# When an edge sum's round reads its register values: needs behind the one-hot rows, places behind the node work

## The reference, cut to what matters

```
edge_index = stack([src, dst])              # 50000 edges, sorted by dst, dst = 50000 * u**2
x = ln(x + EdgeMLP(x))                      # segment_sum(mlp(x[src], x[dst]) * w, dst)          agg0
x = ln(x + Sage2(x))                        # segment_sum(h[src], dst) / deg, twice              agg1, agg2
x = ln(x + Gcn2(x))                         # segment_sum(h[src] * norm, dst), twice             agg3, agg4
x = ln(x + Attention(x))                    # segment_sum(v[src] * softmax_by_src, dest)         agg5
```

## Time and profile before

| | us |
|---|---|
| median of 3 runs | 7158.25 |
| profiled execution | 7164.57 |
| its span | 7162.9 |
| busy in the span: PE / DVE / ACT / POOL | 4883.4 / 4104.0 / 2723.8 / 4236.2 |
| first to last one-hot rows of agg0 | 1186 to 1600 |
| of agg1, agg2 | 1904 to 2426, 2439 to 2946 |
| of agg3, agg4 | 3293 to 3862, 3898 to 4413 |
| of agg5 | 6364 to 6902 |

### The profile page before, as it was taken

One profiled execution on the slowest core, in us unless ns is written; L12 is line 12 of the kernel. 1 busy time (PEld: TensorE's weight loads), 2 busy tenths in 40 slices (PEclk: granted clock), 3 DMA queues, 4 the chain that ended last, 5 costly groups with the idle time before them and its releaser, 6 DMA issues. The chain is left out here.

```text
span 7162.9 us, 132892 instructions
## 1 busy us (share of the span) xinstructions
PE 4883.4 (68%) x26557; PEld 3828.3 (53%) x26558; DVE 4104.0 (57%) x13488; ACT 2723.8 (38%) x6771; POOL 4236.2 (59%) x4642
## 2 busy tenths in 40 slices
PE   4666666779876666796787665766666767436667
PEld 2555554548654455685665554544444444325545
DVE  4555557887785432374454323866666666565448
ACT  1555555317642242495411422921111111113139
POOL 3777772004577777304766776467777777437740
PEclk7777778999997685798898866977777777667569
DMA  1222224649863233696775644932222222124358
GB/s 29 73 74 74 74 73 127 196 147 360 299 195 118 83 123 87 203 331 209 224 236 177 199 134 145 303 97 71 69 70 72 68 71 69 59 68 117 87 173 292
DMA packets 560382, 1016.38 MB, mean 142 GB/s; under 512 B 118514, under 2 KB 127120, under 8 KB 559888
## 3 DMA queue, kind: packets, MB, share of 16 engines
q1 hardware_dynamic: 243536, 444.87, 19.0%
q10 hardware_dynamic: 183456, 334.05, 13.5%
q0 software_dynamic: 133280, 236.29, 13.0%
HBM read 624.60 MB, written 390.17 MB: 142 GB/s over the span
## 5 line engine op out<-in xcount | busy, mean ns | idle before, releaser
L497 PE MATMUL agg_bank<-agg_msgs,agg_onehot 128*128 x7840 | 1404.1, 336 | 601.1 <-DVE agg_onehot L434 465.9
L497 PEld LDWEIGHTS agg_bank<-agg_msgs,agg_onehot 128*128 128x128 f32 x7840 | 1210.1, 236 | 852.9 <-issue 848.3
L434 DVE TENSOR_TENSOR agg_onehot<-iota,rel 128x512 f32<-128x512 f32 x1176 | 814.0, 692 | 1281.5 <-SPq L402 518.3
L356 POOL DMA_INDIRECT agg_msgs<-y,agg_rows x784 | 783.6, 999 | 294.1 <-issue 197.0
L534 ACT ACTIVATE agg_kept<-agg_bank,inv_root 128x128 f32<-128x128 f32 x784 | 223.4, 368 | 751.9 <-PE agg_bank L497 737.4
L534 ACT ACTIVATE agg_kept<-agg_bank,inv_deg 128x128 f32<-128x128 f32 x784 | 223.5, 368 | 693.0 <-PE agg_bank L497 666.4
L353 POOL DMA_INDIRECT agg_weight<-weights,agg_rows x392 | 406.8, 1038 | 127.0 <-issue 100.4
L497 PE MATMUL agg_bank<-agg_weighted,agg_onehot 128*128 x1568 | 338.1, 386 | 209.8 <-DVE agg_onehot L434 160.3
L1176 POOL DMA_INDIRECT mlp_xs<-in_x,mlp_rows x392 | 409.4, 1044 | 116.7 <-issue 115.8
L356 POOL DMA_INDIRECT agg_msgs<-near,agg_rows x392 | 395.1, 1008 | 122.3 <-issue 98.0
L1472 POOL DMA_INDIRECT by_source<-score_line,score_places x392 | 387.7, 989 | 127.3 <-issue 118.7
(11 more groups left out here) (334 smaller groups left out, 12457.6 us busy)
## 6 DMA issues: line engine op xcount, KB each, us to landing
sums<-agg_kept ACTq DMA_DIRECT2D x490, 256.0 KB, 2.1
agg_first<-y ACTq DMA_DIRECT2D x196, 256.0 KB
messages<-mlp_m SPq DMA_DIRECT2D x98, 256.0 KB, 2.1
agg_first<-in_x ACTq DMA_DIRECT2D x98, 256.0 KB
agg_msgs<-messages SPq DMA_DIRECT2D x98, 256.0 KB
l_z<-sums SPq DMA_DIRECT2D x98, 256.0 KB
x<-l_o POOLq DMA_DIRECT2D x98, 256.0 KB
near<-l_near_o SPq DMA_DIRECT2D x98, 256.0 KB
```

What stands on the lines that cost most here:

```text
L356: pool.indirect_dma_start(msgs[:, j, :], None, table[:, :], bass.IndirectOffsetOnAxis(ap=rows[:, third, j:j + 1], axis=0)).then_inc(sm[f"g ...
L434: nc.vector.tensor_tensor(onehot[:, j, :, :], k.iota[:, 0:P].unsqueeze(1).to_broadcast([P, Q, P]), k.rel[:, ds(i * (4 * Q) + j * Q, Q)].un ...
L497: t.matmul(bank[:, column[q], :], onehot[:, j, q, :], messages[:, slot[q], :], start=False, stop=True, skip_group_check=True)\
```

## The change

Two loads of registers stand at another place in the round.

- VectorE reads the needs of round n + 1 directly behind the one-hot rows of round n, in front of tally or node work, in all six edge sums. Round 0's are read ahead of the loop. So `needs` has one round more (16 bytes), is set to zero first, and everything allocated behind it starts 32 bytes later.
- PE, in agg3 alone, reads the places of round n + 1 behind the round's node step instead of ahead of it. In the other five sums it stays where it was.

```diff
+                c.link(v.memset(k.needs[0:1, :, :], 0))
...
-        def quads(eng, body, node_step, lag):
+        def quads(eng, body, node_step, lag, close=None):
...
                 for j in range(4):
                     body(i + FIRST_BESIDE, j)
                     node_step(i, j)
+                    if close is not None:
+                        close(i + FIRST_BESIDE, j)
...
-                def quad(i, j):
-                    dve.reg_load(words, k.needs[0:1, ds(i * 4 + j, 1), 0:len(words)])
+                def read_needs(at):
+                    dve.reg_load(words, k.needs[0:1, at, 0:len(words)])
                     for to, of in zip(least, words):
                         dve.reg_alu(to, of, 1, ALU.max)
+
+                read_needs(0)
+
+                def quad(i, j):
                     arrived = dve.snap(least[0], min_val=1, max_val=ET)
...
                         ALU.is_equal).then_inc(sm["onehot"], 1)
+                    read_needs(ds(i * 4 + (j + 1), 1))
...
+                def read_places(i, j):
+                    for half in (0, Q):
+                        pe.reg_load(regs[half:half + Q], k.places[0:1, ds(i * 4 + (j + 1), 1), half:half + Q])
...
-                    for half in (0, Q):
-                        pe.reg_load(regs[half:half + Q], k.places[0:1, ds(i * 4 + (j + 1), 1), half:half + Q])
+                    if beside is None:
+                        read_places(i, j)
...
-                quads(pe, quad, beside and beside.tensor(pe), beside and beside.LAST)
+                quads(pe, quad, beside and beside.tensor(pe), beside and beside.LAST, read_places)
...
-    k.needs = sb("needs", [1, STEPS // Q, 4], I32)
+    k.needs = sb("needs", [1, STEPS // Q + 1, 4], I32)
```

More of the change, by code:

```diff
@@ L204, in _ @@
                 c.link(v.memset(k.places[0:1, :, :], 0))
+                c.link(v.memset(k.needs[0:1, :, :], 0))
                 c.link(v.tensor_scalar(k.places[0:1, 0:STEPS // Q, 0:Q], es_i[0:1, :].rearrange(quads, q=Q), RING - 1, None, ALU.bitwise_and))
                 c.link(v.tensor_scalar(k.places[0:1, 0:STEPS // Q, Q:2 * Q], ns_i[0:1, :].rearrange(quads, q=Q), BANKS * Q - 1, None, ALU.bitwise_and))
-                c.link(v.tensor_scalar(k.needs[0:1, :, 0:1], es[0:1, :].rearrange(quads, q=Q)[:, :, Q - 1:Q], 1.0, None, ALU.add))
+                c.link(v.tensor_scalar(k.needs[0:1, 0:STEPS // Q, 0:1], es[0:1, :].rearrange(quads, q=Q)[:, :, Q - 1:Q], 1.0, None, ALU.add))
                 c.link(v.tensor_scalar(quad_i[0:1, :].unsqueeze(2), es_i[0:1, :].rearrange(quads, q=Q)[:, :, Q - 1:Q], 2, None, ALU.logical_shift_right))
@@ L212, in _ @@
                 c.link(v.tensor_scalar(quad_i[0:1, :], quad_i[0:1, :], RING // Q - 1, None, ALU.bitwise_and))
-                c.link(v.tensor_copy(k.needs[0:1, :, 2:3], quad_i[0:1, :].unsqueeze(2)))
+                c.link(v.tensor_copy(k.needs[0:1, 0:STEPS // Q, 2:3], quad_i[0:1, :].unsqueeze(2)))
                 c.link(v.tensor_copy(quad[0:1, :], quad_i[0:1, :]))
@@ L219, in _ @@
                 c.link(v.tensor_tensor(quad[0:1, :], quad[0:1, :], begun[0:1, :], ALU.mult))
-                c.link(v.tensor_tensor(k.needs[0:1, :, 3:4], quad[0:1, :].unsqueeze(2), spare[0:1, :].unsqueeze(2), ALU.add))
+                c.link(v.tensor_tensor(k.needs[0:1, 0:STEPS // Q, 3:4], quad[0:1, :].unsqueeze(2), spare[0:1, :].unsqueeze(2), ALU.add))
                 c.link(v.tensor_scalar(es_i[0:1, :], ns_i[0:1, :], 2, None, ALU.logical_shift_right))
                 c.link(v.tensor_copy(tmp[0:1, :], es_i[0:1, :]))
-                c.link(v.tensor_scalar(k.needs[0:1, :, 1:2], tmp[0:1, :].rearrange(quads, q=Q)[:, :, Q - 1:Q], 1.0, None, ALU.add))
+                c.link(v.tensor_scalar(k.needs[0:1, 0:STEPS // Q, 1:2], tmp[0:1, :].rearrange(quads, q=Q)[:, :, Q - 1:Q], 1.0, None, ALU.add))
                 for q in range(4):
@@ L300, in aggregate @@
             beside.allocate(nc, ctx, out, [sm[f"written{u}"] for u in range(BANKS)])
-        def quads(eng, body, node_step, lag):
+        def quads(eng, body, node_step, lag, close=None):
             def one(i, j):
                 body(i, j)
-                if node_step is not None and (not isinstance(i, int) or i >= FIRST_BESIDE):
-                    node_step(i - FIRST_BESIDE, j)
+                node_step(i - FIRST_BESIDE, j)
+                if close is not None:
+                    close(i, j)
             whole, peeled = STEPS // (4 * Q), 0 if node_step is None else 3
@@ L312, in quads @@
                     body(i, j)
+                    if node_step is not None and close is not None:
+                        close(i, j)
             if node_step is None:
```

## The result

| | before | after |
|---|---|---|
| median of 8 runs, us | 7158.87 (7152.95 to 7167.5) | 7136.38 (7125.34 to 7141.14) |
| profiled execution, us | 7164.57 | 7136.26 |
| its span, us | 7162.9 | 7134.6 |
| agg3, first to last one-hot rows, us | 569.3 | 537.4 |
| agg0 / agg1 / agg2 | 414.2 / 521.8 / 506.6 | 413.2 / 520.8 / 508.3 |

The account below looks back on a forecast made before the run. PE's sequencer, late behind its loads, was taken to hold up agg3's node-work stretch: 274 us to 230 + 8 + 15 = 253, 21 less, with 0.7 more in setup, giving 7137 us; range 7112 to 7161.

Parts of the forecast that it names:

- Within 2 us: Sign of being right: the five edge sums other than agg3 keep their lengths within 2 us.
- PE's transposes: agg3's node-work stretch: PE's idle time before the transposes falls from 39.7 us to under 10.
- The branch: agg3's node-work stretch: loop branch, now behind the loads, adds 0.43 us before edge matmuls, 8 us for 19 branches.
- Slow loads: agg3's node-work stretch: loads of places above 0.34 us have 30 us excess, of which 15 shows before edge matmuls.
- Rival 1: The wait only moves: DMA queues keep loads slow, exposed behind the product; gain 6 us, 7153; chance 29%.
- PE busy as a constant 230: agg3's node-work stretch: PE's 230 us of busy time, taken unchanged as the base of the new length.
- One-hot rows: agg3's node-work stretch: PE's 3.4 us wait for them before edge matmuls becomes none after VectorE's load moves.
- VectorE's part: Load behind one-hot rows: rows 0.6 us earlier in agg3's shared stretch; copy late by at most 8 us.
- agg0 and agg1 at no cost: Load ahead of tally rows costs 0, as PE hardly waits; 98 us in agg0 if the cover were gone.
- addresses nothing: Rival: allocations starting 32 bytes later slow transfers; at 30 us the time is 7167; chance 2%.
- The rule on control instructions: Skill's rule: engine instructions can be queued while a control instruction executes; by it the move would gain 0.
- The floor for tensor_load: Skill's 600 ns per load: a pair would take 0.53 us more than covered, 40 us, and the move bring nothing.

Follow-up runs that it names:

- e3: Kernel before with all loads at their old places, only the table of needs one round larger and zeroed in setup; 7158.24 us, ratio 0.9999 to before.
- e5: Kernel before, meant to read places twice at the old place; the repeated loads were missing from what ran, so a repeat of before; 7156.54 us, ratio 1.0000.
- e8: Changed kernel with PE's loads of places between transposes and product instead of behind the product; 7161.53 us, ratio 1.0002 to before.
- e9: Changed kernel with a second, used pair of PE's loads of places behind the product in 96 node-work rounds; 7173.65 us, ratio 1.0009 to before.
- e2: Changed kernel with PE's loads back ahead of the transposes, so only VectorE's loads moved; 7142.38 us, ratio 0.9980 to before.
- e1: Changed kernel with VectorE's loads back at the old place, so only PE's loads moved; 7136.2 us, ratio 0.9963 to before.
- e11: Changed kernel with VectorE reading its needs twice ahead of the tally's rows in agg0 and agg1; 7225.98 us, ratio 1.0081 to before.

## Why the prediction was right, and where its sizes were off

- **Where the gain is, and the other sums.** Right for the place: agg3 got shorter, by 31.9 us between the two traces. Some of that is the trace of before: e3 and e5, of the same order of loads, have 564, so the change is worth some 27 there. The medians say 22.5. Most of the difference is what nobody had priced: 2.6 us in agg1 and 2.7 in agg5, beside the 0.7 in setup. "Within 2 us" did not hold for agg4 (2.6 less) and agg5 (3.3 more).
- **The number, 7137 for 7136.4.** That it is so near is in part luck. In the stretch with node work 253 us were forecast and 241.7 measured: 21 less against 32. The terms below were off by up to 15 us, and the trace of before was a long one. The interval of the measured gain is itself 16 to 32 us.
- **PE's transposes, 39.7 to under 10.** Right, 0.2. e8 shows that the cover does it, the step's own reason; not shorter loads.
- **The branch, 8 us before the edge matmuls.** Nearly: "issue" there is 7.9 us in all, and 5.1 of it stands in the first round behind the branch.
- **Slow loads, 15 us.** Wrong, at most 2.8 us of "issue" are left for them. Loads were 0.74 us a pair in place of 1.12, and a fast pair's path is 1.0 us by e8, where the prediction had 1.3; 1.5 us of queued work covers that. This is most of why rounds take 3.2 us and not 3.4. Rival 1 put the length down to the DMA share; that share rose from 0.79 to 0.85 while the loads shortened, and the rival is out.
- **PE busy as a constant 230.** It was 224.4. But e3 and e5, with the loads at the old place, have 226.3 and 228.0 for the same rounds, and e9, with them and two more at the new place, 230.5. So it varies by some us from trace to trace, and the 6 us can't be put down to the change.
- **One-hot rows, "3.4 us now, none after".** Wrong, 8.3 us. The one-hot rows lost their "issue" of 44.4, as said, but waited 16.0 for gathers. The prediction counted in that POOL "may run into its floor", and gave it no term. PE's 224.4, the 7.9 of "issue" and the 8.3 are 241 of the 241.7 measured.
- **VectorE's part.** The prediction had it as a help to one-hot rows that PE was about to wait for, with at most 8 us against it. Its price was right to leave at nothing (the copy's "issue" is 4.4 us, and doubling the load costs 5). What it gives was not seen: alone 14 us, by the sequencer's lead (e2), beside PE's part nothing (e1). Leaving it out did not spoil the sum, since both parts draw on the same 40 us of idle time.
- **agg0 and agg1 at no cost.** Right in time for agg0 (413.2 us in the mean against 413.6), not quite for agg1 (2.6 more). The reason was wrong. "PE hardly waits" was read from the edge matmuls alone and from one round. The counts of the same stretch, in the trace of before, 1186 to 1600, did wait for the tally rows, 54.3 us:

```profile
L504 PE MATMUL agg_counts<-agg_hot_hi,agg_hot_lo 128*128 128x392 bf16 x388 | 98.0, 335 | 89.3 <-DVE agg_hot_hi L444 54.3 <-issue 35.0
```

  What kept the cost at nothing is that idle time of VectorE only moved from the one-hot to the tally rows. There is little to spare (e11): one more load costs 61 us, 0.31 a round.
- **Setup 0.7 us, the rounds at the end unchanged, addresses nothing.** Right: 0.71 us, 69.7 for 69.2, and e3 at 0.9999.
- **The rule on control instructions** (Trainium skill, Advanced Engine Details and Errata, Sequencer Loop) would let later instructions be queued while a load runs, if a load is a control instruction, which the section doesn't say. e8 is against it with 46.5 us of "issue" behind loads of 0.33. **The floor for tensor_load** (Trainium skill, DMA: Bandwidth & Descriptors, Latency and other measured facts) of about 600 ns doesn't hold as a floor on PE in any of these traces: the shortest are 325 to 328 ns. But for a pair it is not far off in effect, since with its register work each costs the sequencer 0.5 us.

**Open:** why loads are longer ahead of the transposes (1.10 to 1.20 us a pair in before, e2, e3 and e5) than behind them (0.74, and 0.77 in e8). VectorE's own load isn't the reason: it moved in e2 and the pairs kept their length. Which transfers they meet wasn't tried. Also open is why agg1 and agg5 take 2.6 and 2.7 us more.

## What to carry to other kernels

A sequencer's load is hidden by the array work queued in front of it, not by what follows. Put it behind the longest queued group, and count it with its register work: here 1.0 us for a pair whose records say 0.66. And "issue" before one group can be made by another engine, whose late answer cost the sequencer its lead; two changes that both give back lead did not add up here. Before a load is put ahead of work on an engine that looks idle, add up that engine's round, and look at every group that waits for it, not only at the costliest: busy time and gaps of VectorE filled agg0 to the end.

## What the hardware showed that was not expected

- Loads of four words on PE take 0.325 to 0.333 us at best, and two in a row start 0.39 to 0.50 us apart. They were longer ahead of the transposes (up to 1.6 us, in e3) than behind the product, though the DMA share of the stretch was 0.79 at the first place and 0.85 at the second.
- A second pair of loads costs about the same, 31 us, at a place where the engine stood idle for 39.7 us on them and at one where it stood idle for 7.9.
- With node work spread over a stretch the granted clock of the early rounds rose from 0.84 to 0.96, and they still took 24 us longer; that of the late rounds fell from 0.98 to 0.90.
